# A decoder block on one core: the values of cross attention loaded by columns, and single waits moved

## The chip, the cores and the metric

The kernel runs on one core of one Trainium2 chip. The metric is the device time in microseconds (us) of one execution, as the median of several; lower is better. The engines are TensorE (PE, which multiplies matrices and also transposes them), VectorE (DVE), ScalarE (ACT), GpSimd (POOL), and SyncE (SP), whose queue issues the DMA transfers. They run on their own instruction queues, each strictly in order, and meet at semaphores.

## What is computed

Four sequences of 512 rows with 512 columns go through three residual steps:

```
x = x + self_attention(layernorm(x))        # 16 heads of 128, softmax over 512 keys, biases on q, k, v and o
x = x + gamma * cross_attention(layernorm(x), ctx)
x = x + ffn(layernorm(x))                   # weights rounded to three values, silu(h1) * h3, hidden 1365

def cross_attention(q, ctx):                # 8 heads; q, k and v are (batch, 512, 512)
    qh, kh = q.reshape(B, 8, 64, 512), ctx.reshape(B, 8, 64, 512)
    qk = einsum('bhdq,bhdl->bhql', qh, kh) / 8
    return einsum('bhql,bhdl->bhdq', softmax(qk), kh).reshape(B, 512, 512)
```

The context serves both as keys and as values. A head of the cross attention takes 64 rows of both inputs, so the score product needs no transpose (the 64 rows are contracted), but the value product contracts over the 512 columns, so the values must have their columns on the partitions.

## The kernel before

Every matrix product of the attention is made in three passes of 32-bit operands split into a high and a low part: high times high, low times high, high times low. ACT writes a high part (a copy to the reduced format), and DVE or POOL subtracts it from the original to get the low part. Names end in h and l for them (kh and kl, wah and wal, wbh and wbl), or share one buffer (qst holds the high queries in partitions 0 to 63 and the low ones in 64 to 127).

The first 700 us are self attention, in two passes of two batches. In each pass the four groups of heads go through scores (the product M of the K and Q weights with a Gram matrix, L163 to L165, and the scores S) and values. raw_a and raw_b are the weights as loaded; wah and wal are the split of raw_a (K weights in the scores), wbh and wbl that of raw_b (Q weights in the scores, V weights in the values, to which act_bias_v adds a bias first). The second scores hold more: between the products of each group g, at "places" 0 to 8, the kernel runs steps of batch 0's cross attention, called early (tiles whose names begin with e_). Its queue order is written out by hand in functions such as pe_scores_early and dve_scores_early.

The other three batches go through three turns (b = 1, 2, 3), from 737 us on, each beside the FFN of the batch before. A turn is one loop of 32 steps n = 4h + q over 8 heads h and four quarters q of the queries, written out for each engine (pe_turn, act_turn, dve_turn, pool_turn). Step n has: PE the scores of head h, quarter q (pe_sx, L545 and L546); DVE their maximum (L760); ACT the exp (L679); POOL, one step later, the product with 1/sum (pool_prob, L929); PE, four steps later, the transposes of the probabilities (pe_pt, L535), and the value product pe_ret (L557, L558). Between them stand pieces of the FFN: on PE L575 and L576, on ACT th (a tanh) and gth, on POOL gtl (L941). There are two score banks, so PE's score n waits for the exp n - 2.

Ahead of a head's scores comes its preparation, at step prep_step: ACT copies kd to kh (L658) and x1d, normalised by DVE at L744, to qst (L660); POOL makes kl (L919) and the low queries (L923).

```
def prep_step(h): return 4 * h + (h % 4 == 2) if 0 < h < XH - 1 else None   # prepares head h + 1
```

Values are handled for two heads at once, at values_step(h), which is 4h + (h % 4 == 0) for even h and in turn 1, 8, 17, 24: SP loads 128 rows of ctx into vd (L421), PE transposes the four 128 by 128 blocks (pe_vt, L523), ACT writes the high part into vts, DVE the low part (L750). On SP's queue sp_head writes, for each head, first the vd load (even heads only), then two x1d loads (L424) and two kd loads (L425) of half the rows each. The vd load waits for t_ready, the end of PE's transposes of the vd before. The layer norms get 1/sqrt(var) by a chain of 13 dependent small DVE instructions, the first a copy of the variance (L1668), the rest Newton's method (newton_step, L148 to L158).

## Time and profile before

| | before |
|---|---|
| median of 3 runs | 1137.38 us (1136.97 to 1137.83) |
| the profiled execution, its own time | 1134.82 us |
| its span in the trace | 1133.0 us |
| granted TensorE clock | 1.0 of full speed throughout |
| PE busy | 1108.6 us, 98% of the span |
| DVE, ACT, POOL busy | 738.5, 544.8, 469.1 us |
| chain that ended last | PE 92%, DVE 4%, ACT 2%, issue 1% |

All times of rows are microseconds from the start of the span of this one execution, unless marked ns. A row of the timeline has start, duration, engine, line, operation, the tile written and the tiles read, and in brackets how long the engine had been idle and what ended that. SPq is SP's queue as it issues transfers; PEld is the load of weights into TensorE, which overlaps PE. PE's matmuls overlap one another, so the time that one adds is smaller than its own duration.

### The profile page before, as it was taken

The numbers are of one execution on the slowest core, as the hardware profiler recorded it, in microseconds if no ns is written. First come the engines' busy times: TensorE is split into PE (matmuls) and PEld (weight loads), VectorE is DVE, ScalarE is ACT, GpSimd is POOL, SyncE is SP. The second block draws the span as 40 slices with busy tenths as digits, with TensorE's granted clock in tenths as the row PEclk, the third lists the DMA queues.
The fourth block names the chain that finished last, engine by engine and source line by source line (L and its number), as shares of the span: only waits on it lengthen the run. The fifth ranks groups of instructions, "written<-read, shape, count | busy, mean of one in ns | idle before, by whom it ended". The sixth has DMA issues, their size and how long they took to land.

```text
span 1133.0 us, 15861 instructions
## 1 busy us (share of the span) xinstructions
PE 1108.6 (98%) x5824; PEld 938.8 (83%) x5824; DVE 738.5 (65%) x1376; ACT 544.8 (48%) x1129; POOL 469.1 (41%) x412
## 2 busy tenths in 40 slices
PE   5999999999999999999999999999999999999998
PEld 4888888878888878888888888888888888888886
DVE  7555547787757578775524344689968876888532
ACT  3456673324242365676425142267727762776130
POOL 2222326341332265674352140156626752675131
PEclk9999999999999999999999999999999999999999
DMA  7455543544433722412630202462024111410000
GB/s 241 161 187 184 180 163 136 172 124 170 128 118 106 229 92 92 134 39 84 248 112 1 75 20 96 143 211 67 1 81 122 59 47 41 128 47 1 38 1 38
DMA packets 54376, 122.20 MB, mean 108 GB/s; under 512 B 10025, under 2 KB 10025, under 8 KB 52250
## 3 DMA queue, kind: packets, MB, share of 16 engines
q1 hardware_dynamic: 54298, 121.18, 32.7%
q8 instruction: 47, 0.77, 0.3%
q14 instruction: 31, 0.25, 0.1%
HBM read 103.32 MB, written 17.84 MB: 107 GB/s over the span
## 4 chain that ended last, share of the span: by engine, by line
PE 92%; DVE 4%; ACT 2%; issue 1%; DMA 0%; POOL 0%; DVEq 0%; POOLq 0%; SPq 0%
PE bank L163 19%; PE bank L165 19%; PE bank L164 19%; PE bank L575 6%; PE bank L576 6%; PE bank L535 4%; PE bank L590 4%; PE bank L591 4%; PE bank L557 3%; PE bank L558 2%; PE bank L545 2%; PE bank L546 2%; PE bank L600 1%; PE bank L523 0%; DVE xmx L760 0%
## 5 line engine op out<-in xcount | busy, mean ns | idle before, releaser
L575 PE MATMUL bank<-x3h,w 128*128 128x512 f32 (+2 forms) x368 | 143.3, 393 | 0.6 <-DVE x3l L847 0.3
L576 PE MATMUL bank<-x3l,w 128*128 128x512 f32 (+2 forms) x368 | 140.4, 384 | 0.0
L1420 ACT ACTIVATE yh<-bank 128x512 fp32r<-128x512 f32 x64 | 38.1, 600 | 209.9 <-PE bank L165 209.8
L929 POOL TENSOR_SCALAR pe_x<-pe_x,xri,gam 128x512 f32<-128x512 f32 x96 | 76.5, 797 | 99.1 <-DVE xri L764 95.9
L760 DVE TENSOR_REDUCE xmx<-bank 128x1 f32<-128x512 f32 x128 | 87.6, 686 | 30.8 <-PE bank L546 29.1
L1998 POOL TENSOR_TENSOR wal<-raw_a,wah 128x512 fp32r<-128x512 f32 x44 | 60.4, 1402 | 110.8 <-ACT wah L1442 110.8
L163 PE MATMUL bank<-wah,gh 128*128 128x512 f32 x256 | 102.8, 402 | 2.0 <-DVE wal L1728 2.0
L2003 POOL TENSOR_TENSOR wbl<-raw_b,wbh 128x512 fp32r<-128x512 f32 x64 | 87.6, 1396 | 39.0 <-ACT wbh L1462 38.7
L163 PE MATMUL bank<-yh,rh 128*128 128x512 f32 x256 | 100.2, 392 | 0.8 <-DVE xacc L1857 0.8
L163 PE MATMUL bank<-wah,ph 128*128 128x512 f32 x256 | 100.2, 391 | 0.0
L164 PE MATMUL bank<-wal,gh 128*128 128x512 f32 x256 | 100.1, 391 | 0.0
L165 PE MATMUL bank<-wah,gl 128*128 128x512 f32 x256 | 99.9, 390 | 0.0
L164 PE MATMUL bank<-wal,ph 128*128 128x512 f32 x256 | 99.8, 390 | 0.0
L165 PE MATMUL bank<-yh,rl 128*128 128x512 f32 x256 | 99.7, 389 | 0.0
L164 PE MATMUL bank<-yl,rh 128*128 128x512 f32 x256 | 99.7, 389 | 0.0
L165 PE MATMUL bank<-wah,pl 128*128 128x512 f32 x256 | 99.6, 389 | 0.0
L1688 DVE TENSOR_TENSOR yl<-bank,yh 128x512 fp32r<-128x512 f32 x64 | 44.1, 691 | 84.5 <-ACT yh L1420 84.5
L1857 DVE SCALAR_TENSOR_TENSOR xacc<-bank,rinv,xacc 128x512 f32<-128x512 f32 x64 | 47.9, 749 | 69.3 <-PE bank L165 66.9
L679 ACT ACTIVATE pe_x<-bank,xmx 128x512 f32<-128x512 f32 x96 | 66.1, 688 | 34.8 <-DVE xmx L760 34.5
L575 PEld LDWEIGHTS bank<-x3h,w 128*128 128x128 f32 (+1 forms) x368 | 68.2, 185 | 15.1 <-DVE x3l L847 0.7
L576 PEld LDWEIGHTS bank<-x3l,w 128*128 128x128 f32 (+1 forms) x368 | 68.2, 185 | 12.8
L1688 DVE TENSOR_TENSOR ml<-bank,mh 128x512 fp32r<-128x512 f32 x64 | 43.6, 686 | 53.8 <-ACT mh L1420 53.8
(172 smaller groups left out, 2997.8 us busy)
## 6 DMA issues: line engine op xcount, KB each, us to landing
raw_a<-in_wk SPq DMA_DIRECT2D x8, 1024.0 KB, 5.2
raw_b<-in_wq SPq DMA_DIRECT2D x8, 1024.0 KB, 5.6
raw_a<-in_wo SPq DMA_DIRECT2D x8, 1024.0 KB, 5.1
raw_b<-in_wvt SPq DMA_DIRECT2D x8, 1024.0 KB, 4.9
ternary_scratch<-wraw SPq DMA_DIRECT2D x24, 341.2 KB, 3.1
x1d<-x_scratch SPq DMA_DIRECT2D x48, 128.0 KB, 3.0
kd<-in_ctx SPq DMA_DIRECT2D x48, 128.0 KB, 3.2
w<-ternary_scratch SPq DMA_DIRECT2D x2, 2730.0 KB, 10.8
```

What stands on the lines that cost most here:

```text
L163: pe.matmul(out, wh, xh, start=start, stop=False, skip_group_check=shared)
L164: pe.matmul(out, wh, xl, start=False, stop=False, skip_group_check=shared)
L165: return pe.matmul(out, wl, xh, start=False, stop=stop, skip_group_check=shared)
L575: pe.matmul(u_bank[w][0:m, cols], lhs, x3h[:, c, cols], start=c == 0, stop=False)
L576: mm = pe.matmul(u_bank[w][0:m, cols], lhs, x3l[:, c, cols], start=False, stop=c == CK - 1)
L679: act.activation(m.pe_x[:, q, :], m.s[q % 2][:], ACT.Exp, bias=xmx[:, q:q + 1], accum_out=xrs[:, q:q + 1]).then_inc(s["s_free"], 1)
L760: dve.reduce_max(xmx[:, q:q + 1], m.s[q % 2][:], axis=AX, negate=True).then_inc(s["xmx"], 1)
L929: pool.tensor_scalar(m.pe_x[:, q, :], m.pe_x[:, q, :], xri[:, q:q + 1], gam[:], ALU.mult, ALU.mult).then_inc(s["xpn"], 1)
L1688: dve.tensor_tensor(dst, a_bank(u)[:], high.bitcast(F32), ALU.subtract).then_inc(s["a_free"], 1)
L1857: dve.scalar_tensor_tensor(xacc[:, i, a, :], late_bank(n)[:], rinv[:, j, a // 2, q:q + 1], xacc[:, i, a, :], ALU.mult, ALU.add).then_inc(s ...
L1998: pool.tensor_tensor(wal[:, c, :], raw_a[:, c, :], wah[:, c, :].bitcast(F32), ALU.subtract).then_inc(s["wal_pool"], 1)
L2003: pool.tensor_tensor(wbl[:, c, :], raw_b[:, c, :], wbh[:, c, :].bitcast(F32), ALU.subtract).then_inc(s["wbl"], 1)
```

## The change

It has five parts.

1. The host gives a second arrangement of the context, ctx_cols, in which each pair of heads has its columns on the partitions. vd is loaded from it (transfers of the same size), and PE's 16 groups of four transposes (four in the second scores, twelve in the turns) are gone with their PSUM banks. ACT reads vd from SBUF for the high part. In the turns POOL writes the low part (pool_vt, L923 of the changed kernel) and no longer DVE; in the second scores DVE does, from SBUF. A new semaphore vtl counts the low parts. The reload of vd waits for it, and so does the first value product of each pair of heads.
2. In the turns the preparation is spread: ACT's copy of the keys stays at prep_step, its copy of the queries goes behind the exp of the next step, and POOL's two instructions go to the next step too, behind that step's pool_prob.
3. In the second scores, ACT's four exps of the second half of the group before are split in two and two with the high part of a product between them; DVE's split of the next K weights (L1728) comes right behind the last low part of a product; and POOL's preparation of head 2 stands between two halves of pool_add.
4. Where V weights get their bias and split on ACT, the two operations alternate (act_v_parts), part by part.
5. The copy at the head of the Newton chain is gone; its first link reads the variance itself.

```diff
                 gate(sp, "sp")
             if h % 2 == 0 and b > 0:
                 if h or b > 1:
-                    sp.wait_ge(s["t_ready"], t_v(b, h - 2) + 1 if h else t_v(b - 1, XH - 2) + 1)
-                sp.dma_start(m.vd[:], rows(ctx, b)[XD * h:XD * (h + 2), :]).then_inc(s["vd_in"], 16)
+                    sp.wait_ge(s["vtl"], b * V_TILES + h // 2)
+                sp.dma_start(m.vd[:], rows(ctx_cols, b)[h // 2]).then_inc(s["vd_in"], 16)
...
-        def pe_vt(pe, m, b, h):
-            pe.wait_ge(s["vd_in"], b * 16 * V_TILES + 16 * (h // 2 + 1))
-            pe_wait(pe, "t_free", t_v(b, h), m.ring)
-            tb = m.t[t_v(b, h) % 2]
-            for c in range(CK):
-                mm = pe.transpose(tb[:, c * P:(c + 1) * P], m.vd[:, c * P:(c + 1) * P], ident[:])
-            mm.then_inc(s["t_ready"], 1)
...
+            if half == 0 and h % 2 == 0:
+                pe.wait_ge(s["vtl"], b * V_TILES + h // 2 + 1)
...
+            act_keys(act, m, b, h)
+            act_queries(act, m, b, h)
...
+        def act_queries(act, m, b, h):
+            n, slot = b * XH + h, h % 2
             act.wait_ge(s["xq"], n + 1)
             act.activation(m.qst[:, slot, :], m.x1d[:, slot, :], ACT.Copy).then_inc(s["qh"], 1)
...
-        def v_tile(m, b, h):
-            tb = m.t[t_v(b, h) % 2][:].rearrange("p (c e n) -> p e c n", e=2, n=XD)
-            return tb, m.vts[:, h % 4:h % 4 + 2, :, 0:XD], m.vts[:, h % 4:h % 4 + 2, :, XD:P]
+        def v_parts(m, h):
+            slots = slice(h % 4, h % 4 + 2)
+            return m.vd[:].rearrange("p c (e n) -> p e c n", e=2), m.vts[:, slots, :, 0:XD], m.vts[:, slots, :, XD:P]
         def act_vt(act, m, b, h):
-            tb, high, low = v_tile(m, b, h)
-            act.wait_ge(s["t_ready"], t_v(b, h) + 1)
-            act.activation(high, tb, ACT.Copy).then_inc(s["vth"], 1)
+            values, high, low = v_parts(m, h)
+            act.wait_ge(s["vd_in"], 16 * (b * V_TILES + h // 2 + 1))
+            if b == 1 and h < 4:
+                act.wait_ge(s["a_ready"], A["Y", PASSES - 1, GROUPS - 1, 1, CK - 1] + 1)
+            else:
+                act.wait_ge(s["r_ready"], 2 * (b * XH + h - 3) + 2)
+            act.activation(high, values, ACT.Copy).then_inc(s["vth"], 1)
...
-                        act_prep(act, main, b, h + 1)
+                        act_keys(act, main, b, h + 1)
+                    if prep_step(h) == n - 1:
+                        act_queries(act, main, b, h + 1)
...
-        def dve_vt(dve, m, b, h):
-            tb, high, low = v_tile(m, b, h)
-            dve.wait_ge(s["vth"], (b - 1) * V_TILES + (h // 2 + 1))
-            dve.tensor_tensor(low, tb, high.bitcast(F32), ALU.subtract).then_inc(s["t_free"], 1)
...
-                    link(dve.tensor_copy(nvar_b[:], mv_b[:, :, 1]))
                 for m in range(TJ * (k - TJ), TJ * (k - TJ + 1)):
-                    newton_step(dve, link, rstd_b[:], ntmp_b[:], nvar_b[:], m)
+                    newton_step(dve, link, rstd_b[:], ntmp_b[:], nvar_b[:], m, mv_b[:, :, 1])
...
+        def pool_vt(pool, m, b, h):
+            values, high, low = v_parts(m, h)
+            pool.wait_ge(s["vth"], b * V_TILES + h // 2 + 1)
+            pool.tensor_tensor(low, values, high.bitcast(F32), ALU.subtract).then_inc(s["vtl"], 1)
...
                 if b is not None:
                     if n:
                         pool_prob(pool, main, b, (n - 1) // 4, (n - 1) % 4)
-                    if prep_step(h) == n:
+                    if prep_step(h) == n - 1:
                         pool_prep(pool, main, b, h + 1)
+                    if values_step(h // 2 * 2) == n - 1:
+                        pool_vt(pool, main, b, h // 2 * 2)
...
                             pe_t_early(pe, g - 1, 0)
                     if place == 5:
                         pe_s(pe, p, g, 1)
-                        pe_v_early(pe, g)
...
+        def act_v_parts(act, p, step):
+            act_bias_v(act, p, step, range(0, 1))
+            for c in range(1, CK):
+                act_bias_v(act, p, step, range(c, c + 1))
+                act_split_b(act, p, step, range(c - 1, c))
+            act_split_b(act, p, step, range(CK - 1, CK))
...
+            values, high, low = v_parts(early, 2 * g)
+            act.wait_ge(s["vd_in"], 16 * (g + 1))
+            if g >= 2:
+                act.wait_ge(s["r_ready"], 2 * (2 * g - 3) + 2)
+            act.activation(high, values, ACT.Copy).then_inc(s["vth"], 1)
...
+        def act_attention_half(act, p, g, pr, qs=range(4)):
+            if 0 in qs:
+                act.wait_ge(s["nmx"], pair(p, g, pr) + 1)
+            for q in qs:
                 e = act.activation(pw[:, pr, q * P:(q + 1) * P], pair_bank(pr)[:, q * P:(q + 1) * P], ACT.Exp,
                                    bias=nmx[:, pr, q:q + 1], scale=SCALE_A, accum_out=rs[:, g, pr, q:q + 1])
-            e.then_inc(s["s_read"], 1)
+            if 3 in qs:
+                e.then_inc(s["s_read"], 1)
...
                     if n is not None and (place or g == 0):
                         act_early_rows(act, n)
                     act_high(act, mh[:, c % 2, i, :], A["M", p, g, c, i])
+                    if place == 1 and g:
+                        act_attention_half(act, p, g - 1, 1, range(2, 4))
                     if g and 1 <= place <= CK:
                         act_split_b(act, p, g, [place - 1])
                     if place == 2 * CK - 1:
                     if n is not None:
                         act_early_step(act, n)
                     if place == 0 and g:
-                        act_attention_half(act, p, g - 1, 1)
+                        act_attention_half(act, p, g - 1, 1, range(0, 2))
...
                         dve_early_rinv(dve, n)
                         dve_early_max(dve, n)
                     dve_low(dve, ml[:, c % 2, i, :], mh[:, c % 2, i, :], A["M", p, g, c, i])
+                    if place == 2 * CK - 1:
+                        dve_split_a(dve, p, g + 1)
...
-                dve_split_a(dve, p, g + 1)
...
                 if g + 1 == GROUPS:
                     pool_early(pool, early_step(g, 7))
                 if g + 1 < GROUPS:
-                    pool_add(pool, p, g + 1)
+                    pool_add(pool, p, g + 1, range(0, CK // 2))
+                    if g == 0:
+                        pool_prep(pool, early, 0, 2)
+                    pool_add(pool, p, g + 1, range(CK // 2, CK))
...
+        "ctx_cols": np.asarray(ctx_2048).reshape(B, XH // 2, P, CK, P).transpose(0, 1, 4, 3, 2),
```

The first place is POOL's queue in a turn, at steps 6 to 11, before. pe_x are the probabilities of a step, kl and qst the preparation of head 3, gtl the FFN's.

```order
L929 TENSOR_SCALAR pe_x<-pe_x,xri,gam 128x512 [waits s_xrinv] x3
L919 TENSOR_TENSOR kl<-kd,kh 128x512 [waits s_kh]
L923 TENSOR_TENSOR qst<-x1d,qst 64x512 [waits s_kl,s_qh]
L941 TENSOR_TENSOR gtl<-gf,gth 128x512 [waits s_gh2,s_ql]
L929 TENSOR_SCALAR pe_x<-pe_x,xri,gam 128x512 [waits s_xrinv] x3
```

The same stretch of POOL's queue in the changed kernel, where vts is the low part of the values:

```order
L918 TENSOR_SCALAR pe_x<-pe_x,xri,gam 128x512 [waits s_xrinv] x3
L923 TENSOR_TENSOR vts<-vd,vts 128x8x64 [waits s_vth]
L935 TENSOR_TENSOR gtl<-gf,gth 128x512 [waits s_gh2]
L918 TENSOR_SCALAR pe_x<-pe_x,xri,gam 128x512 [waits s_xrinv]
L908 TENSOR_TENSOR kl<-kd,kh 128x512 [waits s_kh]
L912 TENSOR_TENSOR qst<-x1d,qst 64x512 [waits s_kl,s_qh]
L918 TENSOR_SCALAR pe_x<-pe_x,xri,gam 128x512 [waits s_ql,s_xrinv]
```

The preparation of head 3 has moved behind the low part of the values, gtl and one more step's probabilities.

The second place is SP's queue for head 2 of the second turn, before:

```order
L421 DMA vd<-in_ctx 128x512 [waits s_ql,s_t_ready]
L424 DMA x1d<-x_scratch 64x512
L425 DMA kd<-in_ctx 64x512
L424 DMA x1d<-x_scratch 64x512
L425 DMA kd<-in_ctx 64x512
```

And in the changed kernel:

```order
L413 DMA vd<-in_ctx_cols 128x512 [waits s_ql,s_vtl]
L416 DMA x1d<-x_scratch 64x512
L417 DMA kd<-in_ctx 64x512
L416 DMA x1d<-x_scratch 64x512
L417 DMA kd<-in_ctx 64x512
```

Nothing has moved, but the semaphore at the head of the five is another one, raised by POOL and not by PE.

The third place is POOL's queue at the end of group 0 of the second scores, before. raw_b<-raw_b,rowq are the four additions of pool_add, e_kl and e_qst the preparation of head 2.

```order
L2021 TENSOR_TENSOR raw_b<-raw_b,rowq 128x512 [waits s_raw_b,s_row_sum]
L2021 TENSOR_TENSOR raw_b<-raw_b,rowq 128x512 x3
L929 TENSOR_SCALAR e_pe_x<-e_pe_x,xri,gam 128x512 [waits s_xrinv] x2
L919 TENSOR_TENSOR e_kl<-e_kd,e_kh 128x512 [waits s_kh]
L923 TENSOR_TENSOR e_qst<-e_x1d,e_qst 64x512 [waits s_kl,s_qh]
L2003 TENSOR_TENSOR wbl<-raw_b,wbh 128x512 [waits s_wbh,s_ql]
```

And in the changed kernel:

```order
L2017 TENSOR_TENSOR raw_b<-raw_b,rowq 128x512 [waits s_raw_b,s_row_sum]
L2017 TENSOR_TENSOR raw_b<-raw_b,rowq 128x512
L908 TENSOR_TENSOR e_kl<-e_kd,e_kh 128x512 [waits s_kh]
L912 TENSOR_TENSOR e_qst<-e_x1d,e_qst 64x512 [waits s_kl,s_qh]
L2017 TENSOR_TENSOR raw_b<-raw_b,rowq 128x512 [waits s_ql]
L2017 TENSOR_TENSOR raw_b<-raw_b,rowq 128x512
L918 TENSOR_SCALAR e_pe_x<-e_pe_x,xri,gam 128x512 [waits s_xrinv] x2
```

The preparation of head 2 now has two additions and two products with 1/sum less ahead of it.

## Rows read from the trace of the kernel before

**Rows 1.** The page, busy time and share of the span by engine, with instructions:

```profile
PE 1108.6 (98%) x5824; PEld 938.8 (83%) x5824; DVE 738.5 (65%) x1376; ACT 544.8 (48%) x1129; POOL 469.1 (41%) x412
```

**Rows 2.** PE's waits: releaser, us in total, times, longest:

```profile
PE bank L163 <- DVE wal L1728: 2.0, 1, 2.0
PE bank L545 <- POOL e_qst L923: 1.6, 1, 1.6
...
PE bank L163 <- issue: 0.6, 1, 0.6
```

**Rows 3.** Chain of what ended last (start, us): eight transposes; then groups by form:

```profile
91.50 0.87 PE bank L1236 x8
...
L523 PE MATMUL bank<-ident,vd 128*128 128x128 f32 x48 | 7.2, 272 | 0.0
```

**Rows 4.** Timeline of the startup (start, us, engine, line, operation):

```profile
8.01 0.17 DVE L1668 COPY nvar<-mvar 128x4 f32<-128x4 f32 x1
8.21 0.17 DVE L148 TENSOR_SCALAR nvar<-nvar 128x4 f32<-128x4 f32 x1
```

**Rows 5.** Timeline of the second turn, first head (idle time and releaser in brackets):

```profile
851.87 0.34 SPq L421 DMA_DIRECT2D vd<-in_ctx  x1
...
854.02 0.60 SPq L425 DMA_DIRECT2D kd<-in_ctx  x1
...
854.50 0.77 POOL L929 TENSOR_SCALAR pe_x<-pe_x,xri,gam 128x512 f32<-128x512 f32 x1 [1.27 <-DVE xri L764]
...
857.86 0.63 ACT L658 ACTIVATE kh<-kd 128x512 fp32r<-128x512 f32 x1
...
859.17 0.63 ACT L660 ACTIVATE qst<-x1d 128x512 fp32r<-128x512 f32 x1 [0.68 <-DVE x1d L744]
...
860.76 0.69 ACT L679 ACTIVATE pe_x<-bank,xmx 128x512 f32<-128x512 f32 x1
...
861.59 0.50 PE L545 MATMUL bank<-kh,qst 128*128 128x512 f32 x1 [0.53 <-ACT pe_x L679]
```

**Rows 6.** The tile kd: its low part on POOL in ns, and its loads:

```profile
L919 POOL TENSOR_TENSOR kl<-kd,kh x24: 1278/1292/1299, 715.7 to 1025.9; 128x512 fp32r<-128x512 f32 x24
...
DMA to landing us min/median/max: 2.6/3.2/11.0
```

**Rows 7.** Timeline of the second turn, steps 17 to 23:

```profile
893.32 0.34 SPq L421 DMA_DIRECT2D vd<-in_ctx  x1
...
897.21 0.77 POOL L929 TENSOR_SCALAR pe_x<-pe_x,xri,gam 128x512 f32<-128x512 f32 x1 [1.75 <-DVE xri L764]
...
900.86 0.62 ACT L658 ACTIVATE kh<-kd 128x512 fp32r<-128x512 f32 x1
...
902.38 0.69 ACT L679 ACTIVATE pe_x<-bank,xmx 128x512 f32<-128x512 f32 x1
...
905.05 0.49 PE L545 MATMUL bank<-kh,qst 128*128 128x512 f32 x1
```

**Rows 8.** Timeline of the second turn, steps 8 to 12:

```profile
869.89 0.68 DVE L750 TENSOR_TENSOR vts<-bank,vts 128x512 fp32r<-128x512 f32 x1
...
872.11 0.89 POOL L929 TENSOR_SCALAR pe_x<-pe_x,xri,gam 128x512 f32<-128x512 f32 x1 [3.11 <-DVE xri L764]
...
874.40 1.29 POOL L923 TENSOR_TENSOR qst<-x1d,qst 64x512 fp32r<-64x512 f32 x1
...
875.77 1.31 POOL L941 TENSOR_TENSOR gtl<-gf,gth 128x512 fp32r<-128x512 f32 x1
...
876.92 0.39 PE L545 MATMUL bank<-kh,qst 128*128 128x512 f32 x1
```

**Rows 9.** Timeline of the second turn, steps 25 to 28:

```profile
918.32 0.15 DVE L764 RECIPROCAL xri<-xrs 128x1 f32<-128x1 f32 x1
...
920.43 0.39 PE L545 MATMUL bank<-kh,qst 128*128 128x512 f32 x1
```

**Rows 10.** The tile x1d: durations in ns, least, median and greatest:

```profile
L744 DVE TENSOR_SCALAR x1d<-x1d,stx x24: 527/530/1280, 717.2 to 1024.8; 128x512 f32<-128x512 f32 x24
```

More of the change, by code:

```diff
@@ L99, in attention_banks @@
     for n, key in enumerate(attention_tiles()):
-        early = key[0] == "M" and key[1] == PASSES - 1 or key[0] in "TV" or key[:4] == ("Y", PASSES - 1, 0, 0)
+        early = key[0] == "M" and key[1] == PASSES - 1 or key[0] == "T" or key[:4] == ("Y", PASSES - 1, 0, 0)
         allowed = range(RING_A - 1 if early else RING_A)
@@ L133, in early_step @@
     return n if n >= 0 else None
-RSTD_STEPS = 1 + 12
+RSTD_STEPS = 12
 X1_STEPS = RSTD_STEPS + 2
@@ L374, in prep_step @@
             return 4 * h + (h % 4 == 2) if 0 < h < XH - 1 else None
-        def t_v(b, h):
-            return b * T_TILES - V_TILES + max(0, values_step(h) - 3) + h // 2
         def t_p(b, h, q):
-            if b == 0:
-                return 4 * h + q
-            return b * T_TILES - V_TILES + 4 * h + q + sum(values_step(v) < 4 * (h + 1) + q for v in range(0, XH, 2))
+            return b * T_TILES + 4 * h + q
         def t_x3(b, t):
@@ L616, in pe_turn @@
                             pe_up(pe, f, piece)
-                    if b is not None and h % 2 == 0 and values_step(h) == 4 * h + q:
-                        pe_vt(pe, main, b, h)
             if b is not None:
@@ L833, in dve_x3 @@
             link(i)
-            link(dve.tensor_copy(nvar_b[:], mv_b[:, :, 1]))
-            for k in range(RSTD_STEPS - 1):
-                newton_step(dve, link, rstd_b[:], ntmp_b[:], nvar_b[:], k)
+            for k in range(RSTD_STEPS):
+                newton_step(dve, link, rstd_b[:], ntmp_b[:], nvar_b[:], k, mv_b[:, :, 1])
             assert count[0] == LINK_B, count
@@ L1246, in pe_t_early @@
             mm.then_inc(s["a_ready"], 1)
-        def pe_v_early(pe, g):
-            u = A["V", g]
-            pe.wait_ge(s["vd_in"], 16 * (g + 1))
-            pe_bank(pe, u)
-            for c in range(CK):
-                mm = pe.transpose(a_bank(u)[:, c * P:(c + 1) * P], early.vd[:, c * P:(c + 1) * P], ident[:])
-            mm.then_inc(s["a_ready"], 1)
         def pe_early_scores(pe, n):
@@ L1442, in act_split_a, with act_bias_v @@
                 act.activation(wah[:, c, :], raw_a[:, c, :], ACT.Copy).then_inc(s["wah"], 1)
-        def act_bias_v(act, p, step):
-            act.wait_ge(s["dv"], GROUPS * p + step - GROUPS + 1)
-            for c in range(CK):
+        def act_bias_v(act, p, step, cs=range(CK)):
+            if 0 in cs:
+                act.wait_ge(s["dv"], GROUPS * p + step - GROUPS + 1)
+            for c in cs:
                 act.activation(raw_b[:, c, :], raw_b[:, c, :], ACT.Identity, bias=dv[:, c:c + 1]).then_inc(s["vadd"], 1)
@@ L1477, in act_t_early @@
             act.activation(ptf[:, g, pr, :], a_bank(u)[:], ACT.Copy).then_inc(s["att_free"], 1)
-        def v_tile_early(g):
-            tb = a_bank(A["V", g])[:].rearrange("p (c e n) -> p e c n", e=2, n=XD)
-            slots = slice(2 * g % 4, 2 * g % 4 + 2)
-            return tb, early.vts[:, slots, :, 0:XD], early.vts[:, slots, :, XD:P]
         def act_v_early(act, g):
-            tb, high, low = v_tile_early(g)
-            act.wait_ge(s["a_ready"], A["V", g] + 1)
-            act.activation(high, tb, ACT.Copy).then_inc(s["a_hi"], 1)
-        def act_attention_half(act, p, g, pr):
-            act.wait_ge(s["nmx"], pair(p, g, pr) + 1)
-            for q in range(4):
+            values, high, low = v_parts(early, 2 * g)
[7 more added lines that the diff above has]
+            for q in qs:
                 e = act.activation(pw[:, pr, q * P:(q + 1) * P], pair_bank(pr)[:, q * P:(q + 1) * P], ACT.Exp,
                                    bias=nmx[:, pr, q:q + 1], scale=SCALE_A, accum_out=rs[:, g, pr, q:q + 1])
-            e.then_inc(s["s_read"], 1)
+            if 3 in qs:
+                e.then_inc(s["s_read"], 1)
         def act_attention(act, p, g):
@@ L1780, in dve_v_early @@
         def dve_v_early(dve, g):
-            tb, high, low = v_tile_early(g)
-            dve.wait_ge(s["a_hi"], split(A["V", g]))
-            dve.tensor_tensor(low, tb, high.bitcast(F32), ALU.subtract).then_inc(s["a_free"], 1)
+            values, high, low = v_parts(early, 2 * g)
+            dve.wait_ge(s["vth"], g + 1)
+            dve.tensor_tensor(low, values, high.bitcast(F32), ALU.subtract).then_inc(s["vtl"], 1)
         def dve_early_values(dve, link, n):
@@ L2014, in pool_scores, with pool_add @@
                 pool_split_b(pool, p, g + 1)
-        def pool_add(pool, p, g):
-            pool.wait_ge(s["row_sum"], g)
-            pool.wait_ge(s["raw_b"], 16 * (load(p, g) + 1))
-            for c in range(CK):
+        def pool_add(pool, p, g, cs):
+            if 0 in cs:
+                pool.wait_ge(s["row_sum"], g)
+                pool.wait_ge(s["raw_b"], 16 * (load(p, g) + 1))
+            for c in cs:
                 pool.tensor_tensor(raw_b[:, c, :], raw_b[:, c, :], rowq[:, 0, :], ALU.add).then_inc(s["wadd_b"], 1)
```

42 lines of the change are left out of this document (18 added, 24 removed).

## The prediction, made before the changed kernel ran

> **What bounds the kernel now.** I read the page first. TensorE (PE) is busy 98% of the span [rows 1], so nearly every microsecond lies on its queue, and the change can be worth only three things: work of PE that goes, waits of PE that go, and new waits. The list of PE's waits [rows 2] is short: two for the second scores that this change touches, 2.0 and 1.6 us, and one put down to the issue of its own instructions, 0.6 us. So there is little to remove, and the question is how near PE already runs to its suppliers in the turns. For that I went through the timeline of one turn, the second (848 to 950 us). A turn has 32 steps n = 4h + q, and the same code runs in all three.
>
> **What it takes off PE.** The transposes of the values: 16 groups of 4, 64 instructions. Eight transposes of the same size in a row take 0.87 us of the chain [rows 3], 0.109 us each, so 64 are worth 7.0 us. The busy time of the 48 in the turns is 7.2 us, 0.15 each [rows 3]; at that price 64 are 9.6 us, but this counts the filling of the array, which overlaps the neighbour, so 9.6 is the upper bound.
>
> The Newton copy: in the startup each link of the DVE chain begins 0.20 us after the one before [rows 4], and PE waits for the end of this chain. One link less is 0.2 us. In the turns the same link lies beside PE's work: nothing.
>
> The second scores: the split of the K weights of the next group is moved ahead of other DVE work (2.0 us of wait), the preparation of head 2 is taken out from behind the last two 1.3 us additions on POOL, as the rows of the order show (1.6 us), and the interleaved bias and split of the V weights feeds POOL one part earlier (the 0.6 us at the first values). Between 0 and 4.2 us; I take all of it, plus 0.3 for a short wait on DVE that follows the same late head, 4.5 in all. The low part of the early values stays on DVE, and the high part on ACT reads SBUF as kh does, 0.63 us [rows 5]; both have work of PE over them, so they cost nothing here. Savings: 7.0 + 0.2 + 4.5 = **11.7 us**.
>
> **What it costs: the load of the values in SP's queue.** The buffer vd is single. Before, its reload waited for PE's transposes; now it waits until POOL has made the low part, and the x1d and kd loads of the same head are issued behind it (the order of SP). For head 2 of the second turn the vd load went out at 851.87 [rows 5]. Now POOL does step 1's probabilities first, at about 854.1 (854.50 [rows 5] less the 0.44 of PE's own transposes), 0.77 us, and then the low part. No row has that instruction; POOL's two-input operation on the same number of elements takes 1.29 us [rows 6], and I take that (the lower bound would be the 0.77 of POOL's one-input operation). So vd goes out at 854.1 + 0.77 + 1.29 = 856.2, 4.3 us later. The last kd load goes out 2.15 us behind it (854.02 - 851.87) and lands 3.2 us later [rows 6]: 861.5. ACT copied that kd into kh at 857.86 [rows 5], 857.4 with the transposes gone. ACT's queue is in order: behind the kh copy stand a gate activation, a probability copy and the exp of step 5. That exp began 2.90 us behind kh (860.76 - 857.86), of which the queries' copy, now moved behind it, took 0.68 of waiting for DVE and 0.63 of its own: 1.6 us are left. So the exp starts at 863.1 and ends at 863.8, where it ended at 861.45. PE needs it for the scores two steps on, which ran at 861.59 after already waiting 0.53 [rows 5]; without the transposes that would be 861.15. They now run at about 863.85, **2.7 us later**. Bounds: 2 us (the low part at 0.77, the lower end) to 4 us (a landing a microsecond slower than the median) per turn. Three turns: 8.1.
>
> Head 6 has the same arrangement. Its vd went out at 893.32; now behind the probabilities of step 17 (897.21 less 0.44 and less the 0.60 that DVE saves, 0.77 long) and 1.29: at 898.3, 5.0 later. kd lands at 898.3 + 2.15 + 3.2 = 903.65. The exp of step 21 began 1.52 us behind kh (902.38 - 900.86 [rows 7]), of which some 0.5 was the queries' copy; so it starts at 904.66 and ends near 905.4. The scores of step 23 stood at 905.05, 904.6 without transposes: **0.8 us per turn**, 0 to 1.5, three turns 2.4. For head 4 the same working ends just before ACT's copy of its keys, so I count nothing there.
>
> **What it costs: the order of POOL.** Preparation is one step later, behind that step's probabilities, and behind the low part where there is one. For head 3 (the order of POOL, steps 9 and 10) three things now stand ahead of kl: the low part 1.29, gtl 1.31 which moved ahead, with 0.1 of dispatch, and the probabilities 0.77, together 3.46. DVE gives back 0.60 of its 0.68 low part [rows 8], since the probabilities at 872.11 were waiting for DVE. The low queries ended at 874.40 + 1.29 = 875.69; now 875.69 + 3.46 - 0.60 - 0.44 = 878.1. PE's scores of head 3 begin at 876.92 - 0.44 = 876.5: **1.6 us** per turn, bounds 1 to 2, three turns 4.8. In front of it there was a reserve of 1.23 us, so this one doesn't depend on the exact price of the low part.
>
> For head 7 the preparation now stands behind the probabilities of step 25, whose reciprocal comes at 918.32 [rows 9], 917.28 with the 0.60 and 0.44 off. Then 0.35 to the start of POOL, 0.77, and 2.72 for kl and the low queries (1.29 each and the gap between): 921.1. The scores stood at 920.43, 919.9 less the same 0.44 and the 0.1 that a shorter queue gives: **1.2 us**, 0.5 to 1.5, three turns 3.7.
>
> **Sum.** -11.7 + 8.1 + 2.4 + 4.8 + 3.7 = +7.3 us. The profiled execution took 1134.82; this gives 1142.1. The median of the runs, 1137.38, stands 2.56 above that execution, so the forecast is **1144.7 us**.
>
> **A rule against the change.** The normalisation of x1d on DVE, one and the same instruction 24 times, takes 0.53 us mostly and 1.28 at the longest [rows 10]. So something holds an instruction of DVE now and then by 0.75 us, and POOL is the engine that works on the same memory beside it. The Trainium skill, "SBUF — State Buffer", section "Who interferes with whom", states that DVE and GpSimd share one port pair as an exclusive lock. By that rule, work moved from DVE to POOL is also time in which DVE can be shut out, and the sum would be that of the last rival below; by the sum above the move costs only POOL's own time. The trace agrees in this row as far as a hold of this size exists.
>
> **Rivals.**
> - *The order of POOL hides, the loads do not.* For it: both heads start from a reserve. Against: it is 1.23 us at head 3, and 2.9 more stand on POOL (3.46 - 0.60). Then -11.7 + 10.5 = -1.2, 1136.2 us.
> - *The loads hide, POOL's order bites.* For it: landing ranges from 2.6 us up. Then -11.7 + 8.5 = -3.2, 1134.2 us.
> - *The other side: neither bites.* The mechanism is the reserve on PE's own queue. Every step has FFN pieces, which run while a score is awaited; if these pieces stretch far enough over the late instructions of ACT and POOL, PE never sees them. It decides at head 2: kd must land by about 858.3 (857.4 and the 1.3 of the moved queries, less the 0.5 that PE waits now), so vd must go out by 853, before POOL's low part can start. For it: only three short waits of this kind exist now. Against: the instants worked out above. 1137.4 - 11.7 = 1125.7; with 9.6 for the transposes 1123.
> - *The lock costs more.* Each of the 12 low parts on POOL holds one DVE instruction by the 0.75 us that x1d shows (1.28 - 0.53), on the path every time: 12 x 0.75 = 9.0 more, 1153.7 us.
>
> **How the numbers follow.** What can be told from no change is 0.2%, 2.3 us. Forecast 0.60 (its own range 1140 to 1149: the four costs have bounds of 10.5 to 27 us together, the savings of 7.2 to 14.3, and I leave out the quarter at either end, where all would fall to one side); only loads 0.12; only POOL 0.08; neither 0.14; the lock 0.06. Faster holds neither, and most of only-POOL: 0.22. Same holds only-loads and a little of the forecast, 0.13. Slower 0.65. The range for 8 in 10 goes from 1131 to 1150.
>
> **What would show it.** In the changed profile: no transposes of vd on PE; PE busy less by 5 to 9 us but the span longer; among PE's waits new rows of L545's line with ACT's exp near 2.7 us three times and with POOL's low queries 1.2 to 1.6 us six times; vd issues of heads 2 and 6 four to five microseconds later against the scores; POOL near 485 us busy, DVE some 8 lower; the 2.0 and 1.6 us waits gone. Wrong if kd of head 2 lands before ACT reaches its copy, if the low part runs in well under 1 us, or if PE's waits in the turns stay at tenths.

## The result and the profile after

The changed kernel takes 1152.15 us (median of 4 runs, 1148.46 to 1153.28) where before took 1137.18 beside it: a ratio of 1.0127, interval 1.0115 to 1.0139. Slower, as forecast, but by twice the forecast, and outside the range (1131 to 1150).

The profiled execution took 1152.31 us, 17.5 more than the one of before; its span is 1150.4 us. Its page, busy time by engine, answers to [rows 1]:

```profile
PE 1109.9 (96%) x5760; PEld 938.4 (82%) x5760; DVE 730.1 (63%) x1353; ACT 542.1 (47%) x1129; POOL 482.6 (42%) x424
```

PE is busy 1.3 us longer although 64 transposes are gone. Its waits, which answer to [rows 2] (releaser, us in total, times, longest), say where the span went:

```profile
PE bank L529 <- ACT pe_x L675: 11.8, 7, 3.6
PE bank L529 <- POOL qst L912: 7.2, 6, 1.4
PE bank L543 <- DVE x L768: 2.2, 3, 0.9
```

The waits on wal, e_qst and issue are gone. In their place stand 21 us of waits for the exps of ACT (11.8), the low queries of POOL (7.2) and DVE, which frees the value products' bank (2.2). To see where they lie I cut both traces at the first scores of each turn (the third turn ends at those of its step 31). The columns are the stretch, its length, the busy time of PE, PEld, DVE, ACT and POOL with their instructions, the granted clock, DMA share and GB/s. In the trace of before the same stretches are 110.45, 109.70 and 79.40 us long, the first begins at 737.87 and the clock is 1.00 in each.

```profile
731.69:850.82 119.13, 111.83 (x611) 93.78 (x610) 92.63 (x211) 65.28 (x142) 64.18 (x63) 0.97 0.27 84
850.82:967.88 117.06, 110.10 (x611) 92.54 (x610) 84.52 (x175) 65.57 (x143) 66.44 (x67) 0.99 0.21 64
967.88:1054.87 86.99, 79.79 (x446) 66.92 (x444) 65.04 (x131) 57.35 (x127) 56.47 (x58) 0.98 0.21 61
```

The first turn begins 6.2 us earlier (731.69 against 737.87). Then the turns lose 8.7, 7.4 and 7.6 us. What lies behind them is as long as before. So the early gain is there in full, and everything else is in the turns; and one number is new: the granted clock, 1.00 in the profiled execution of before, is 0.97 to 0.99.

**The first head.** The timeline of the changed kernel's second turn, which starts 2.50 us later in the span than before's (850.82 against 848.32); it answers to [rows 5]:

```profile
856.77 0.77 POOL L918 TENSOR_SCALAR pe_x<-pe_x,xri,gam 128x512 f32<-128x512 f32 x1 [1.04 <-DVE xri L757]
...
857.51 1.29 POOL L923 TENSOR_TENSOR vts<-vd,vts 128x512 fp32r<-128x512 f32 x1
...
858.83 0.34 SPq L413 DMA_DIRECT2D vd<-in_ctx_cols  x1
...
860.98 0.60 SPq L417 DMA_DIRECT2D kd<-in_ctx  x1
...
864.68 0.63 ACT L645 ACTIVATE kh<-kd 128x512 fp32r<-128x512 f32 x1 [4.37 <-DMA kd<-in_ctx]
...
866.26 0.69 ACT L675 ACTIVATE pe_x<-bank,xmx 128x512 f32<-128x512 f32 x1
...
867.09 0.50 PE L529 MATMUL bank<-kh,qst 128*128 128x512 f32 x1 [3.60 <-ACT pe_x L675]
```

The chain stands there as the prediction had it. The low part takes 1.29 us, vd goes out right at its end, 4.5 us later than before against the turn's start (6.96 - 2.50), ACT sits 4.37 us with nothing to do until kd lands, and PE then 3.60 us until the exp is done. Two things are worse than worked out. The last kd takes 3.70 us from issue to ACT's start, not the 3.2 of the median. And the wait is followed by something:

```profile
864.00:867.00 3.00, 0.00 (x0) 0.00 (x0) 1.60 (x3) 2.32 (x6) 0.00 (x0) 1.00 1.01 378
868.00:871.00 3.00, 3.00 (x14) 2.81 (x13) 2.51 (x6) 2.50 (x7) 2.79 (x3) 0.50 0.21 49
```

In the 3 us before it starts again PE does nothing; in the 3 us from 868 it runs at a granted clock of 0.50, the lower of its two levels (1.2 GHz); from 872 on it is at 1.00 again. This happens four times in the turns:

```profile
748.00:752.00 4.00, 4.00 (x19) 3.57 (x17) 3.19 (x9) 2.86 (x7) 3.61 (x4) 0.57 1.04 347
796.00:800.00 4.00, 3.82 (x14) 3.46 (x15) 3.57 (x10) 2.16 (x6) 3.77 (x4) 0.57 0.00 0
867.00:872.00 5.00, 4.91 (x20) 4.35 (x21) 3.51 (x9) 3.50 (x9) 4.13 (x5) 0.66 0.33 74
983.00:988.00 5.00, 4.10 (x17) 3.72 (x18) 4.35 (x10) 4.38 (x11) 3.32 (x4) 0.66 0.62 166
```

The first, third and fourth stand behind the wait at step 7 of each turn (2.71, 3.60 and 3.34 us), the second behind two waits of 0.85 and 0.94 us, some 2 us apart, at head 6 of the first turn. The time missing at full clock is 4 x 0.43, 4 x 0.43, 5 x 0.34 and 5 x 0.34: 6.8 us, or 1.7 us each. Over the whole span the clock has a mean of 0.994. So it has in two of the other three executions (1152.00 and 1153.28 us); the fourth has 0.997, half the missing time, and is the shortest, 1148.46 us.

**Head 3**, steps 9 to 12 of the same turn (answers to [rows 8]):

```profile
878.94 1.29 POOL L923 TENSOR_TENSOR vts<-vd,vts 128x512 fp32r<-128x512 f32 x1
...
880.19 1.28 POOL L935 TENSOR_TENSOR gtl<-gf,gth 128x512 fp32r<-128x512 f32 x1
...
881.47 0.76 POOL L918 TENSOR_SCALAR pe_x<-pe_x,xri,gam 128x512 f32<-128x512 f32 x1
...
882.20 1.28 POOL L908 TENSOR_TENSOR kl<-kd,kh 128x512 fp32r<-128x512 f32 x1
...
884.95 0.50 PE L529 MATMUL bank<-kh,qst 128*128 128x512 f32 x1 [1.25 <-POOL qst L912]
```

POOL has no gap between these four. The reciprocal that L918 needs came from DVE at 880.87, and L918 began at 881.47, when gtl was done.

**Head 6** (answers to [rows 7]): vd goes out 55.6 us from the start of the turn, where it was 45.0 before (893.32 - 848.32). The scores of head 3 had lost 5.5 by then (34.1 against 28.6), so 5.1 are the load's own, as forecast. ACT's copy waits 3.30 us for kd, and PE waits twice, for the exp and then for DVE to free the value products' bank.

```profile
906.42 0.34 SPq L413 DMA_DIRECT2D vd<-in_ctx_cols  x1
...
911.47 0.63 ACT L645 ACTIVATE kh<-kd 128x512 fp32r<-128x512 f32 x1 [3.30 <-DMA kd<-in_ctx]
...
913.31 0.50 PE L529 MATMUL bank<-kh,qst 128*128 128x512 f32 x1 [0.38 <-ACT pe_x L675]
...
915.05 0.35 PE L543 MATMUL bank<-pxh,vts 128*128 128x256 f32 x1 [0.57 <-DVE x L768]
```

### The profile page after: what moved, and what is told of

It reads as the page before. It is cut to its first block, busy times and chain, and to the rows that moved or that the text cites. A ratio compares the mean times of both kernels' runs of the same rounds, so it can differ in the third digit from the quotient of the medians.

```text
span 1150.4 us, 15714 instructions
## 1 busy us (share of the span) xinstructions
PE 1109.9 (96%) x5760; PEld 938.4 (82%) x5760; DVE 730.1 (63%) x1353; ACT 542.1 (47%) x1129; POOL 482.6 (42%) x424
## 4 chain that ended last, share of the span: by engine, by line
PE 81%; DVE 6%; POOL 4%; DMA 3%; issue 2%; ACT 2%; SPq 1%; POOLq 0%; DVEq 0%; ACTq 0%
PE bank L161 18%; PE bank L162 18%; PE bank L163 18%; PE bank L561 4%; PE bank L562 4%; PE bank L577 4%; PE bank L576 4%; PE bank L519 3%; PE bank L543 2%; PE bank L544 2%; PE bank L529 2%; PE bank L530 1%; POOL pe_x L918 1%; POOL qst L912 1%; POOL vts L923 1%
## 5 line engine op out<-in xcount | busy, mean ns | idle before, releaser
L918 POOL TENSOR_SCALAR pe_x<-pe_x,xri,gam 128x512 f32<-128x512 f32 x96 | 75.1, 783 | 109.8 <-DVE xri L757 106.3
```

The lines of the kernel that those rows point to most:

```text
L918: pool.tensor_scalar(m.pe_x[:, q, :], m.pe_x[:, q, :], xri[:, q:q + 1], gam[:], ALU.mult, ALU.mult).then_inc(s["xpn"], 1)
```

## The experiments

Each is timed in rounds beside the kernel before (1136.9 us median in both sets). Diffs are against the changed kernel unless they are said to be against the one before. Each computes the whole block.

**1. The vd load behind the keys.** One move in sp_head:

```diff
-            if h % 2 == 0 and b > 0:
-                if h or b > 1:
-                    sp.wait_ge(s["vtl"], b * V_TILES + h // 2)
-                sp.dma_start(m.vd[:], rows(ctx_cols, b)[h // 2]).then_inc(s["vd_in"], 16)
             for half in range(2):
                 part = slice(XD * half, XD * (half + 1))
                 sp.dma_start(m.x1d[part, slot, :], rows(x1_dram, b)[XD * h:XD * (h + 1), :]).then_inc(s[f"x1d_in{slot}"], 16)
                 sp.dma_start(m.kd[part, slot, :], rows(ctx, b)[XD * h:XD * (h + 1), :]).then_inc(s[f"kd_in{slot}"], 16)
+            if h % 2 == 0 and b > 0:
+                if h or b > 1:
+                    sp.wait_ge(s["vtl"], b * V_TILES + h // 2)
+                sp.dma_start(m.vd[:], rows(ctx_cols, b)[h // 2]).then_inc(s["vd_in"], 16)
```

> The changed kernel, but with the reload of vd issued behind the x1d and kd loads of its head on SP's queue, so that the keys no longer stand behind POOL's low part of the values. Theory (the queue): the waits of PE for the exp at step 7 (about 3.5 us in each turn) and near steps 21 to 23 (about 1.5 us) go, and with them the stretches of about 3.4 us at a granted clock of 0.5 behind them (1.7 us lost in each, four in the trace): 3 x 3.5 + 3 x 1.5 + 4 x 1.7 = 22 us less, near 1130 us, clock 1.0. Rival (POOL's and DVE's own time: the low part on POOL holds up what runs beside it, and the loads only look late): the waits stay near two thirds of what they are, 1145 us or more.

Measured 1132.30 us (1131.86 to 1134.12), ratio to before 0.9962 (0.9947 to 0.9977), clock 1.0 in the profile. 19.9 us less by the place of one kind of load in a queue. PE's waits in its profile:

```profile
PE bank L529 <- POOL qst L912: 7.7, 6, 1.9
...
PE bank L529 <- ACT pe_x L675: 0.2, 1, 0.2
```

The exps' 11.8 us are down to 0.2; the low queries' are nearly what they were. Between the two traces, 1150.4 and 1130.7 us long, the exps' waits give 11.6, those for the value products' bank 0.9 (2.2 and 1.3) and the clock 6.8: 19.3 of the 19.7 us. The rival, that POOL's work itself stretches everything, falls.

**2. The preparation back.**

```diff
-                        act_keys(act, main, b, h + 1)
-                    if prep_step(h) == n - 1:
-                        act_queries(act, main, b, h + 1)
+                        act_prep(act, main, b, h + 1)
...
-                    if prep_step(h) == n - 1:
+                    if prep_step(h) == n:
                         pool_prep(pool, main, b, h + 1)
```

> The changed kernel with the preparation in the turns back where it was: ACT's copy of the queries right behind the keys, POOL's two instructions at prep_step, ahead of the low part of the values. Theory (POOL's order costs by itself): PE's six waits for POOL's low queries (7.2 us in all) go; the copy of the queries stands ahead of the late exp of step 5 again, some 0.6 us in each turn more. About 1152 - 7.2 + 1.8 = 1147 us, clock still 0.994. Rival (the order is only late because the loads made everything late): below 0.2% of change, 1150 to 1154 us.

Measured 1158.98 us (1156.96 to 1161.35), ratio 1.0200 (1.0183 to 1.0217): neither; it is 6.8 us slower. The waits for the low queries are gone as the theory said, but those for the exps grew from 11.8 to 16.0 us, those for the bank from 2.2 to 3.8, and the mean clock is 0.990, some 12 us missing where the changed kernel lacks 6.8:

```profile
PE bank L529 <- ACT pe_x L675: 16.0, 9, 3.4
...
PE bank L543 <- DVE x L766: 3.8, 6, 1.0
```

The rows at head 3 of the second turn show why:

```profile
882.75 1.29 POOL L910 TENSOR_TENSOR qst<-x1d,qst 64x512 fp32r<-64x512 f32 x1
...
884.12 1.30 POOL L921 TENSOR_TENSOR vts<-vd,vts 128x512 fp32r<-128x512 f32 x1
...
885.44 0.34 SPq L413 DMA_DIRECT2D vd<-in_ctx_cols  x1
...
890.53 0.63 ACT L645 ACTIVATE kh<-kd 128x512 fp32r<-128x512 f32 x1 [2.29 <-DMA kd<-in_ctx]
```

The low part of head 2's values now stands behind kl and the low queries, so vd goes out 31.9 us from the turn's start (853.51) instead of 29.4 (880.25 - 850.82), and kd of head 4, which in the changed kernel came just in time, is late too: ACT waits 2.29 us. The two parts of the change are tied: as long as the loads hang on POOL's low part, whatever stands ahead of it on POOL is paid again in the next loads.

**3. Both.** The edits of 1 and 2 together.

> The changed kernel with both: vd issued last and the preparation back. Theory: what is left of the change is its savings, 6.2 us before the first turn (as the trace of the changed kernel shows) and 0.3 to 0.44 us for each of the 12 groups of transposes in the turns, so 1137.2 - 6.2 - 4 to 5 = about 1126 us, and no wait of PE above 1 us in the turns. Rival (POOL's low part costs through what it shares with DVE): 1130 us or more, with longer DVE instructions beside the low part.

Measured 1125.13 us (1124.86 to 1125.38), ratio 0.9896 (0.9881 to 0.9910): 27.0 us faster than the changed kernel and 11.8 faster than before, the fastest of all. The longest waits of PE that are left in the turns:

```profile
PE bank L519 <- POOL pe_x L916: 0.7, 1, 0.7
PE bank L543 <- DVE x L766: 0.7, 1, 0.7
```

Its turns, cut in the same way, are 0.1, 2.0 and 1.9 us shorter than before's:

```profile
732.28:842.62 110.34, 108.69 (x611) 91.24 (x610) 94.10 (x211) 65.24 (x142) 64.55 (x63) 1.00 0.30 91
842.62:950.32 107.70, 107.49 (x611) 91.03 (x610) 84.67 (x175) 66.13 (x143) 66.97 (x67) 1.00 0.23 69
950.32:1027.78 77.46, 77.25 (x446) 65.46 (x444) 65.19 (x131) 57.89 (x127) 56.96 (x58) 1.00 0.24 69
```

**4. The low part on DVE again.**

```diff
+        def dve_vt(dve, m, b, h):
+            values, high, low = v_parts(m, h)
+            dve.wait_ge(s["vth"], b * V_TILES + h // 2 + 1)
+            dve.tensor_tensor(low, values, high.bitcast(F32), ALU.subtract).then_inc(s["vtl"], 1)
...
                     dve_max(dve, main, b, h, q)
+                    if values_step(n // 4 // 2 * 2) == n - 1:
+                        dve_vt(dve, main, b, n // 4 // 2 * 2)
...
-                    if values_step(h // 2 * 2) == n - 1:
-                        pool_vt(pool, main, b, h // 2 * 2)
```

> The changed kernel with one part undone: the low part of the values in the turns is made by DVE again, from SBUF, at the place in its queue where it was before. Theory: DVE can make it about 2.6 us earlier than POOL does in the first head of a turn, so kd lands about 2.6 us earlier, PE's wait at step 7 shrinks from 3.5 to 1 us, and the clock does not fall; head 3's preparation has 1.3 us less ahead of it on POOL but DVE works 0.6 longer, head 7's stays: 1152 - 3 x 2.6 - 3 x 1.4 - 4 x 1.7 - 2 + 1.5 = about 1133 us. Rival (who makes the low part doesn't matter, the new order of the preparation does): 1147 us or more.

Measured 1140.14 us (1139.45 to 1141.87), ratio 1.0033 (1.0022 to 1.0045). The direction is the theory's, 7 us short of its size. The exps' waits shrank as worked out, but the low queries' grew from 7.2 to 10.8, where I had expected those of head 3 to shrink, and the clock did fall once, between 1035 and 1039 us (0.57, 1.7 us missing). That is behind a wait of 1.88 us for the low queries; three others of 1.87 and 1.88 us in the same trace have no drop behind them.

```profile
PE bank L529 <- POOL qst L919: 10.8, 6, 1.9
PE bank L529 <- ACT pe_x L675: 1.9, 4, 0.8
```

**5. Both, with the low part on DVE.** The edits of 1, 2 and 4.

> The version with vd issued last and the preparation back (measured at 1125.1 us), now with the low part of the values in the turns made by DVE from SBUF instead of POOL. Theory (which engine makes it is worth little once nothing waits behind it): 1125 to 1127 us; PE's two waits of 0.7 us in the first turn change places. Rival (POOL's low part shuts DVE out, and that is on the path): 1123 us or less.

Measured 1126.89 us (1126.79 to 1128.11), ratio 0.9914 (0.9900 to 0.9927). This is the theory's size. With nothing waiting behind it, the low part on DVE is 1.8 us slower than on POOL, not faster as the rival had it; no execution of the one is as fast as the slowest of the other, but the intervals of the two ratios overlap, so the 1.8 us are no more than likely.

**6. The small parts alone.** The kernel before with parts 3, 4 and 5 of the change, so among others:

```diff
-                    pool_add(pool, p, g + 1)
+                    pool_add(pool, p, g + 1, range(0, CK // 2))
+                    if g == 0:
+                        pool_prep(pool, early, 0, 2)
+                    pool_add(pool, p, g + 1, range(CK // 2, CK))
```

> The kernel before with only the parts of the change that touch neither the values nor the turns' preparation: the moves in the second scores, the alternating bias and split of the V weights, and the shorter Newton chain. Theory: the waits of 2.0, 1.6, 0.6 and 0.3 us go and the chain is 0.2 shorter, 4.7 us less, 1132.2 to 1132.5 us. Rival (the 6.2 us gained before the first turn are mostly the transposes, and the waits go elsewhere): 1135 us or more.

Measured 1131.57 us (1129.97 to 1132.03), ratio 0.9954 (0.9939 to 0.9969): 5.3 us less than before, near the theory and far from the rival. In its trace (the execution of 1129.97 us) the first turn begins at 732.70, 5.2 us earlier.

**7. The later preparation alone.** The kernel before with act_keys and act_queries apart and POOL's preparation a step later (the edit of 2 the other way round).

> The kernel before with only the preparation in the turns spread over two steps, as in the changed kernel; values, loads and transposes as before. Theory (POOL's order costs by itself): on the rows of before, head 3's low queries end 2.2 us later (gtl 1.4 and a probabilities step 0.8 moved ahead) against a reserve of 1.23, a wait of about 1.0; head 7's end at 922.2 against 920.4, 1.7; the copy of the queries no longer delays the exp of step 5, 0.3 to 0.7 us less. Three turns: 8 less 1.5, about 1143 us. Rival (it only costs with the low part of the values on POOL): within 0.2% of before.

Measured 1146.86 us (1146.08 to 1147.66), ratio 1.0087 (1.0073 to 1.0101): 10 us slower, with no low part on POOL at all. PE waits 10.2 us for the low queries, six times:

```profile
PE bank L545 <- POOL qst L931: 10.2, 6, 1.9
```

At head 3 of its second turn:

```profile
878.30 1.28 POOL L949 TENSOR_TENSOR gtl<-gf,gth 128x512 fp32r<-128x512 f32 x1
...
880.24 0.15 DVE L772 RECIPROCAL xri<-xrs 128x1 f32<-128x1 f32 x1
...
880.61 0.78 POOL L937 TENSOR_SCALAR pe_x<-pe_x,xri,gam 128x512 f32<-128x512 f32 x1 [1.02 <-DVE xri L772]
...
884.10 0.50 PE L545 MATMUL bank<-kh,qst 128*128 128x512 f32 x1 [1.67 <-POOL qst L931]
```

gtl ends at 879.58, and POOL then waits a microsecond for the reciprocal of the next step before it may start kl. So without the low part kl starts no earlier: it stands behind the next step's reciprocal. In the changed kernel the two limits lie close together. There POOL's stack ends last, but by only some 0.2 us: the reciprocal at 880.87 with the 0.37 us from its start to POOL's, as here (880.24 to 880.61), gives 881.24, against 881.47.

The trace has one more thing. Its second scores are those of before, and there, where nothing was changed, stand

```profile
452.15 0.47 PE L163 MATMUL bank<-wah,gh 128*128 128x512 f32 x1 [1.95 <-DVE wal L1736]
...
453.00:457.00 4.00, 4.00 (x12) 3.13 (x11) 2.52 (x7) 1.94 (x9) 1.41 (x2) 0.57 0.74 261
```

the wait for wal and behind it a drop of the clock, 1.7 us again. The profiled execution of before has the same wait, 1.97 us, and no drop.

**8. One late load.** As in experiment 1, but for one head in one turn vd is issued first as in the changed kernel:

```diff
-            if h % 2 == 0 and b > 0:
+            if h % 2 == 0 and b > 0 and (b, h) == (2, 2):
                 if h or b > 1:
                     sp.wait_ge(s["vtl"], b * V_TILES + h // 2)
...
+            if h % 2 == 0 and b > 0 and (b, h) != (2, 2):
+                if h or b > 1:
+                    sp.wait_ge(s["vtl"], b * V_TILES + h // 2)
+                sp.dma_start(m.vd[:], rows(ctx_cols, b)[h // 2]).then_inc(s["vd_in"], 16)
```

> The version with vd issued last and the preparation as in the changed kernel (measured at 1132.3 us, clock 1.0), but for head 2 of the second turn alone vd is issued first again. This measures the price of one such wait. Theory: PE waits 3.6 us once, at that step 7, and the granted clock falls to 0.5 for about 3.4 us behind it, 1.7 us lost: 1132.3 + 3.6 + 1.7 = about 1137.5 us. Rival (the clock falls only where several such waits follow one another through the turns): clock 1.0 there, about 1135.9 us.

Measured 1138.78 us over 11 runs (1136.34 to 1139.85), ratio 1.0010 (1.0001 to 1.0019). The second turn, between its first scores and those of the third, is 114.88 us long (846.97 to 961.85) where experiment 1 has 110.08: 4.8 us for one load's place. PE's wait at that step is 2.93 us, and microsecond by microsecond behind it the granted clock (the number behind POOL's) reads:

```profile
863.00:864.00 1.00, 1.00 (x7) 0.91 (x6) 1.00 (x3) 1.00 (x4) 1.00 (x2) 0.61 1.01 186
864.00:865.00 1.00, 1.00 (x6) 1.00 (x6) 1.00 (x3) 1.00 (x4) 0.98 (x1) 0.50 0.94 160
865.00:866.00 1.00, 1.00 (x5) 0.98 (x5) 0.99 (x3) 0.91 (x3) 0.87 (x1) 0.50 0.39 66
866.00:867.00 1.00, 1.00 (x4) 0.77 (x3) 0.00 (x0) 0.07 (x1) 0.76 (x2) 0.69 0.18 64
```

0.61, 0.50, 0.50, 0.69, with 1.00 ahead and behind: the missing time is 1.7 us, and 2.93 + 1.7 is nearly the whole 4.8. The drop needs no series of waits. The profiled execution has a second drop in the first turn, behind a wait for the low queries of 1.9 us that experiment 1 has in the same place with no drop behind it; so there the clock falls in some executions and not in others. The 11 executions bear this out: five have a mean clock of 0.998 and take 1136.34 to 1137.91 us, six have 0.996 or 0.997 and take 1138.78 to 1139.85. This is in the 6.5 us between the medians of experiments 8 and 1 too.

## Why the prediction was wrong in size

**Before the first turn** it was right: 6.4 us forecast (0.2 + 4.5 and 1.7 for the four groups), 6.2 measured; experiment 6 puts 5.2 of it on the small parts, so these gave 0.5 more and the four groups of transposes some 0.7 less than their terms, as far as single executions can tell.

**The transposes in the turns** were taken at 0.44 us a group, 5.2 us for the twelve. The turns of experiment 3 are 0.1, 2.0 and 1.9 us shorter than before's, 4.0 in all. The group at step 2 gave nothing, which I had not seen: counted from the start of the turn, the scores of step 2 begin at 3.53, 3.27 and 3.28 us before and at 3.52, 3.23 and 3.23 in experiment 3, since PE now stands there until the exp of step 0 is done. In the second and third turn the old waits of 0.5 us at step 7 go with it; in the first, two waits of 0.74 and 0.66 us that before does not have took the gain back.

**SP's queue, heads 2 and 6**, was the right mechanism: experiment 1 alone, which undoes it, gives back 19.9 us. Its terms were 8.1 + 2.4 = 10.5. The step that failed is the price of the wait: "They now run at about 863.85, 2.7 us later", and the sum took this for all that a late load costs. How late the scores come was nearly right. PE waited 2.71, 3.60 and 3.34 us at step 7 of the three turns, 9.65 in all; 0.53 and 0.55 of that it had waited there before, which leaves 8.6 against the 8.1 (in the second turn the last kd took 0.5 us over the median to reach ACT). What the prediction put at nothing, without a reason, is the clock behind such a wait: a granted clock of 1.0 throughout was a row of the table of before, and I took it for a property of the kernel. It fell four times, 6.8 us, two thirds of the 10.2 us by which the profiled execution overran the 1142.1 of the sum. Experiments 1 and 3, which take the long waits away, show no such drop in the turns; experiment 8, which puts one back, shows it. Head 6 was mis-sized beside it: its waits were 1.8, 0.95 and 1.4 us in the three turns (0.85 and 0.94; 0.38 and 0.57; 0.73 and 0.67), 4.1 and not 2.4, because the second of each pair, for DVE to free the value products' bank behind the late exp, I had not followed.

**What makes up the 10.2 us:** the clock 6.8, head 6 1.7, step 7 0.5, the transposes in the turns 1.2 if they are taken from experiment 3, the time before the first turn 0.2, and POOL's order 1.3 the other way. That is 9.1; the last 1.1 us I cannot place.

**The 2.56 us added for the median** were a fall of the clock too, as it seems. Of 24 executions of before timed beside the experiments, 22 have a mean clock of 0.998 or 0.999 and take 1135.91 to 1137.92 us; the two at 1.000 take 1134.75 and 1134.92, as the profiled one did (1134.82). One drop of 1.7 us in 1135 is a mean of 0.9985. Where it lies in before is not shown. The wait of 1.97 us for wal is the likely place: experiment 7 has the drop there, and experiment 6, where that wait is gone, ran at 1.000 three times of four. So the kernel before is not free of this either, and of the 11.8 us by which experiment 3 beats it some 2 are the clock's: the two traces at full clock are 9.6 us apart (1133.0 and 1123.4).

**POOL's order, heads 3 and 7**: 1.6 and 1.2 us a turn were forecast, 8.5 in all. The list of waits has 7.2 for the six, and between experiments 1 and 3 it is 7.2 us. The size was nearly right and the reason for head 3 half of it. The sum added up what stands ahead of kl, and in the changed kernel's trace this stack does end last. But experiment 7 has neither the low part nor its 1.29 us and waits longer (10.2 us); experiment 4, with DVE doing 0.7 us more, too (10.8). kl stands behind the next step's probabilities, these behind that step's reciprocal on DVE, and where the stack is shorter it is this that comes last. For head 7 the prediction had argued so; for head 3 it had not.

**The rivals.** "Neither bites" and the two halves are refuted by experiments 1 to 3. The lock was put at 0.75 us for each low part, always on the path; experiments 3 and 5 differ by 1.8 us the other way, so it is not what cost the time. The row that it was priced by, one normalisation of x1d held to 1.28 us [rows 10], has no like in the changed kernel, where DVE's 24 take (ns, least, median, greatest)

```profile
L742 DVE TENSOR_SCALAR x1d<-x1d,stx x24: 527/532/548, 711.0 to 1040.5; 128x512 f32<-128x512 f32 x24
```

The extra time that the range lacked came mostly from the clock, for which there was no rival. The range was also narrower than its own rule: costs of 10.5 to 27 less savings of 7.2 to 14.3 on 1137.4, with a quarter left out at either end, are 1139.5 to 1151.3 and not 1140 to 1149; the measured median is still outside.

**The rule on the shared ports** is borne out by a row, with the price elsewhere. In experiment 3, in the first turn, one of the small instructions of the Newton chain, whose durations on this tile are (ns, least, median, greatest)

```profile
L152 DVE TENSOR_TENSOR ntmp<-rstd x21: 142/163/1147, 8.7 to 799.7; 128x4 f32<-128x4 f32 x18, 128x8 f32<-128x8 f32 x3
```

reads:

```profile
784.08 1.29 POOL L933 TENSOR_TENSOR gtl<-gf,gth 128x512 fp32r<-128x512 f32 x1
...
784.44 0.95 DVE L152 TENSOR_TENSOR ntmp<-rstd 128x4 f32<-128x4 f32 x1
```

It has two inputs in SBUF and ends at 785.39, just as POOL's gtl does (785.37). The Trainium skill, "SBUF — State Buffer", section "Who interferes with whom", says that a DVE instruction with two SBUF inputs contends with one of GpSimd that reads SBUF, over a lock, and that the order of issue decides which of them blocks. The trace agrees: POOL's began 0.36 us earlier, and the two end within 0.02 us of each other. That this decides between experiments 3 and 5 is not shown.

**Left open:** why kd takes 3.7 us to land at head 2 (the DMA engines are fully busy there, a share of 1.01 in the window above, with the load of x that is issued behind it; nothing was run on it), and from which length of a wait on the clock falls. It fell behind the step 7 waits of all three turns (2.71, 3.60 and 3.34 us) and behind that of experiment 8 (2.93). Behind waits near 1.9 us it fell now and then: at 1.87 us in experiment 8 and not in experiment 1, at 1.95 in experiment 7 and not at 1.97 in before, at one of four in experiment 4.

## What to carry to other kernels

When a wait on an in-order queue changes its releaser, follow not the load that waits but the ones queued behind it: here the keys had nothing to spare while the next values are read only some 16 us later (858.83 to 874.72 at head 2 of the second turn), and moving the one that can wait to the end was worth 19.9 us. Where two engines hand work round (POOL's low part frees the load, the load feeds POOL's preparation), undoing one part alone may make it worse; try the pair. And price a wait of TensorE above its own length once it comes near 3 us: in the turns every one of 2.7 us or more cost about 1.7 us on top where its clock was read, and those near 1.9 us did in some executions.

## What the hardware showed unexpectedly

A single wait of 2.9 us on TensorE, in a kernel that otherwise keeps it busy 97% of the time, was followed by 3.4 us at a granted clock of about 0.5, so 1.7 us more than the wait itself (experiment 8: 4.8 us in all). Waits of 1.9 to 2.0 us had this behind them in some executions only, and the runs of experiment 8 spread accordingly, 1136.3 to 1139.9 us. So a mean clock that is short by 0.002 can be most of a spread of 2 us between executions of one kernel, as with the kernel before. A DVE instruction of 0.16 us took 0.95 beside one of POOL.

The clock column does not show everything. PE's first matmuls in the trace of before, from 14.01 to 16.7 us, begin 0.43 us apart and those behind them 0.23, the ratio of the two levels, yet the column reads 1.00 for 14 to 18 us.
